# Block transposes of a cross-attention batch moved from steps 8 and 12 to steps 13 and 21

## The reference

```
x = layernorm(x + self_attention(x))            # 4 heads of 64
x = layernorm(x + cross_attention(x, ctx))      # 16 query heads of 128, 8 key heads, 1500 keys of width 128
x = layernorm(x + mixture_of_experts(x))        # 8 experts, 2 chosen, and a shared one
```

```
scores[h, q, s] = q[h, q, :] . k[h, s, :] / sqrt(128), masked      # 16 heads x 56 queries = 896 rows, 1500 keys
out             = softmax(scores) @ v, then a projection with Wo
```

## Time and profile before

| | |
|---|---|
| runs shown | 1952.05 and 1953.82 us, median 1952.93 |
| profiled execution | 1952.05 us, span 1950.2 us |
| mean granted TensorE clock | 0.93 |
| busy, share of the span | PE 85%, DVE 61%, ACT 53%, POOL 49% |
| DMA | 291.22 MB, 149 GB/s on average; queue of SP 53.3% of 16 engines |

### The profile page before, as it was taken

The page is one execution under the profiler, slowest core; times in us unless marked ns, Lnnn a source line. Parts: engine busy times, 40 slices in busy tenths (PEclk is TensorE's granted clock), DMA queues, the critical chain, the costliest instruction groups (busy, mean ns, idle before and its releaser), DMA issues.

```text
span 1950.2 us, 26771 instructions
## 1 busy us (share of the span) xinstructions
PE 1661.2 (85%) x8882; PEld 1431.6 (73%) x8882; DVE 1199.1 (61%) x3102; ACT 1033.4 (53%) x1780; POOL 946.3 (49%) x790
## 2 busy tenths in 40 slices
PE   8999788787979797878797878797988897869896
PEld 7988677676767676767676767676767676758896
DVE  5556665666666666666666666566666666547447
ACT  5443465655555555555555556555555555434452
POOL 1210354555555555555555555555555555344635
PEclk9999899999989898989898989898999898989999
DMA  4335866666666666666666666666676665533333
GB/s 174 114 129 181 197 162 154 162 154 160 157 158 157 160 158 158 156 162 158 159 152 157 155 153 157 152 157 152 157 153 157 152 158 124 135 127 105 102 97 101
DMA packets 171973, 291.22 MB, mean 149 GB/s; under 512 B 44702, under 2 KB 138560, under 8 KB 171712
## 3 DMA queue, kind: packets, MB, share of 16 engines
q1 hardware_dynamic: 129904, 266.49, 53.3%
q10 hardware_dynamic: 38912, 14.80, 3.2%
q0 software_dynamic: 3024, 8.26, 1.6%
HBM read 189.11 MB, written 100.38 MB: 148 GB/s over the span
## 4 chain that ended last, share of the span: by engine, by line
DMA 28%; PE 19%; POOL 14%; DVE 11%; issue 7%; ACT 6%; SPq 4%; ACTq 0%; DVEq 0%; POOLq 0%
DMA p_store<-b_by_block 26%; POOL b_keyed_over L1247 9%; POOL b_c_raw_over L1235 4%; DVE b_by_block L1093 3%; SPq L796 3%; DVE b_pT_lo L1098 2%; ACT b_p L975 2%; DVE b_p L1072 2%; PE b_turn L882 2%; PE b_score L868 2%; PE b_score L870 2%; PE b_score L869 2%; PE b_out L916 2%; PE c_gate L1647 2%; ACT b_pT_hi L961 2%
## 5 line engine op out<-in xcount | busy, mean ns | idle before, releaser
L1072 DVE CUSTOM_DVE_ANT_0 b_p<-b_score,b_mask_add 128x500 f32<-128x500 f32 x672 | 450.5, 671 | 358.4 <-PE b_score L870 237.3
L1247 POOL TENSOR_TENSOR b_keyed_over<-b_keyed,b_pT_hi 125x384 fp32r<-125x384 f32 x372 | 367.8, 1010 | 481.4 <-ACT b_pT_hi L968 480.9
L961 ACT CAST b_pT_hi<-b_turn 125x512 fp32r<-125x512 f32 x384 | 224.1, 585 | 366.4 <-PE b_turn L882 346.7
L900 PE MATMUL b_out<-b_pT_hi,b_c_hi 125*128 125x512 f32 x384 | 193.5, 504 | 208.8 <-DVE b_pT_lo L1098 208.7
L975 ACT ACTIVATE b_p<-b_p,b_shift 128x1500 f32<-128x1500 f32 x224 | 347.2, 1550 | 24.6 <-DVE b_top_min L1081 24.6
L968 ACT CAST b_pT_hi<-b_keyed 125x384 fp32r<-125x384 f32 x384 | 187.4, 507 | 234.3 <-PE b_out L902 121.8
L1098 DVE TENSOR_TENSOR b_pT_lo<-b_turn,b_pT_hi 125x512 fp32r<-125x512 f32 x384 | 264.0, 688 | 61.5 <-ACT b_pT_hi L961 61.0
L868 PE MATMUL b_score<-b_cT_hi,b_q_hi 128*128 128x500 f32 x672 | 275.3, 410 | 9.3 <-issue 7.5
L869 PE MATMUL b_score<-b_cT_lo,b_q_hi 128*128 128x500 f32 x672 | 272.1, 405 | 0.0
L870 PE MATMUL b_score<-b_cT_hi,b_q_lo 128*128 128x500 f32 x672 | 270.7, 403 | 0.0
L1093 DVE STREAM_TRANSPOSE b_by_block<-b_p 128x1536 f32<-128x1536 f32 x96 | 170.1, 1771 | 132.4 <-DMA p_store<-b_by_block 132.4
(11 more groups left out here) (261 smaller groups left out, 3242.0 us busy)
## 6 DMA issues: line engine op xcount, KB each, us to landing
p_store<-b_by_block SPq DMA_DIRECT2D x384, 192.0 KB, 8.8
b_keyed<-p_store SPq DMA_DIRECT2D x96, 768.0 KB, 14.5
cT_in<-in_ctxT SPq DMA_DIRECT2D x32, 750.0 KB, 7.0
b_c_raw<-in_ctx SPq DMA_DIRECT2D x32, 750.0 KB
q_store<-a_fold_in_or_q_stage SPq DMA_DIRECT2D x16, 896.0 KB, 4.2
q_in<-q_store SPq DMA_DIRECT2D x32, 448.0 KB, 17.9
b_rden_all<-rden_store ACTq DMA_DIRECT2D x32, 256.0 KB, 8.7
b_rden_all<-rden_store ACTq DMA_DIRECT2D x32, 192.0 KB, 6.5
```

The source lines that it names most:

```text
L900: pe.matmul(out, hi, pT_hi[:, c % 3, 0:w], start=(c == 0), stop=False)
L961: act.copy(pT_hi[:, c % 3, 0:w], turn_bank[c % 3][0:CK, 0:w]).then_inc(hi_done, 1)
L1072: dve.tensor_tensor_reduce(out=row(m, u)[:, keys], in0=score_bank[j][:, 0:FW], in1=mask_add[:, b, keys], scale=1.0, scalar=-3.0e38, op0=AL ...
L1247: pool.tensor_tensor(keyed_chunk(keyed_lo, c), keyed_chunk(keyed, c), by_blocks(pT_hi[:, c % 3, 0:128 * EVEN]).bitcast(F32), ALU.subtract) ...
```

## The change

The second and third transposes of a batch stand at steps 13 and 21 of VectorE's stream, where they stood at 8 and 12. The first stays at step 5. On SP the store of the third unit, `store_p(m, 2)`, stands behind the loads of the context and mask two batches ahead, and behind the store of a finished pair and the load of the residual, where it stood in front of all of these. No instruction is added or removed, and all shapes stay.

```diff
@@ phase_b
-        BLOCKS_AT = (5, 8, 12)
+        BLOCKS_AT = (5, 13, 21)
@@ sync(sp), in the loop over m
                 if m:
                     store_p(m, 1)
-                store_p(m, 2)
                 if m + 2 < B:
                     load_cT(m + 2)
                     load_mask(m + 2)
                 if m % 2 and m >= 3:
                     store((m - 3) // 2)
                     residual((m - 1) // 2)
+                store_p(m, 2)
```

## The result

The changed kernel takes **1839.19 us** (median of two runs, 1832.9 to 1845.48) against 1952.93: a ratio of 0.9418 with the 95% interval 0.9278 to 0.9557. The forecast was 1841. On another chip the pair gave 0.9394 [0.9368, 0.9421]. The kernel before differs by up to 2.4% between them, and another kernel need not differ by the same share, so ratios from different chips are not compared more finely than that.

What follows compares the result with a forecast made beforehand. The bound was taken as a cycle of waits, chiefly unit 2's transpose at step 12 on unit 0's late store. Plain batches 92 plus projecting 45 minus transposes 26 gave 111 us off 1952.05: 1841 us, range 1785 to 1905.

Steps and rivals of the forecast that it cites:

- The wait at step 12: VectorE's transpose of unit 2 waiting for unit 0's store to free its buffer; 132.4 us over all transposes, taken to zero.
- Plain batches: Even m: period from 47.6 to 41.5 us, 6.1 us in each of 15, 92 us gained before the transposes' cost.
- Projecting batches: Odd m, 48 more matmuls in steps 9 to 12: period 47.6 to 44.4 us, 45 us in 14 batches.
- rival A: `cT` lands late in projecting batches and takes their gain; 1886 us, or 1918 with transposes more exposed; 17%.
- t: Time in us since SP issues a batch's three `keyed` loads; one such issue to the next is one batch.
- What decides in plain batches: ScalarE's rounding of `c_raw` (L1007, step 15), waiting for its DMA: after t = 22.7, `c_raw` coming 0.9 us earlier.
- Unit 2's store: On SP before the third `keyed` load: lands in 3.2 us, about 2 us before that load wants it.
- Rival B: Unit 2's store lands late (17.6 us), delaying the third `keyed` load; decides from t = 6.1; period 54.0, 2138 us; 7%.
- The moved transposes: 64 transposes at steps 13 and 21 cost 0.9 us a batch (bounds nothing to 3.5), 26 us in 29 batches.
- L900's wait: TensorE standing for a late last `pT_lo`, 208.7 us before; to fall under a quarter, with one at L916 instead.
- Rival C: The wait moves with the transpose, or another fixed stretch keeps the period; 1945 us; 5%.
- rival D: All waits close and TensorE alone bounds: 40.2 us a period, 1737 us; 5%.

Runs made afterwards that it cites:

- the second profile: The changed kernel run once more, unaltered, on another chip: 1797.46 us, ratio 0.9394 to the kernel before.
- `cT` early: Against the changed kernel, the loads of `cT` and the mask also moved ahead of unit 1's stores: 1834.78 us, ratio 0.9611 to the kernel before.

## Why the prediction was right, and where it was not

**The wait at step 12 goes: right.** 132.4 us became 0.3, and moving the third transpose is enough for it. The order alone leaves 101.9 us of it (on another chip).

**Plain batches: right in size.** With the share of the transposes the working put them at 42.4 us; they took 41.7, and 39.7 in the second profile. From the first, 15 x 5.94 = 89 us of the gain.

**Projecting batches: too hopeful by a third.** Put at 45.3 with the transposes, they took 46.0, a gain of 14 x 1.6 = 22 us and not 32 (45.2 in the second profile). Here rival A's mechanism is at work: in the batch shown `cT` is issued at t = 32.4 (the working had about 31), lands 11.8 us later, and ScalarE waits. The working knew both landings, 6.6 and 12.3, said that the cover was thin, and left the wait out of the sum. A's price, though, was 45 us; with the wait taken away (`cT` early) they take 44.9, so as an estimate across chips it costs 1.1 x 14 = 15 us in the first profile and 0.3 x 14 = 4 in the second. The two kinds' errors, 89 us against 15 x 5.2 = 78 and 22 against 32, cancel in the periods, which is luck and no merit of the working. Outside them the first issue came 5.4 us later than before, and the profiled executions differ by 1952.05 - 1845.48 = 106.6.

**What decides in plain batches: right number, wrong route.** The rounding of `c_raw` was to start at t = 22.7; in the batch shown it starts 22.6 us after the first `keyed` issue. But not because `c_raw` has more room: SP issues it at t = 7.9 and no longer at 1.4. The announced sign failed: L1007's wait for `c_raw` was to grow over 50.8 us, and it fell to 12.7 us in 11 waits. In the batch shown `c_raw` is taken 1.0 us earlier in its period than in the earlier trace rows (t = 22.6 for 23.6), and ScalarE is ready for it 1.7 us later (t = 22.0 for 20.3); what keeps ScalarE back was not singled out.

**Unit 2's store: the step that failed.** The working had it land 3.2 us after its last issue and 2 us before SP wants it. In the batch shown it lands after 11.0, and the third `keyed` load is 7.0 us behind the first on average (1.4 before). The rule named in "DMA: Bandwidth & Descriptors" of the Trainium skill, section Specifications, on transfers under 512 B, pointed to this, and the trace agrees as to the place. As the explanation the rule does not do: runs of 12, 16 and 128 bytes are under 512 B too, and with them the late landings are gone. Rival B's price did not follow, though its point was passed: the third load at t = 7.0 is past t = 6.1, and B's sum, 7.0 + 41.5, would make a period of 48.5 us; it is 43.8. B shifted everything behind the load by its full lateness. But `c_raw`, issued 6.5 us later than before, lands in 14.7 us, and took some 22 before (issued 1.3 us behind 1033.92, taken at 1057.48), so that nothing of the lateness is left at its rounding. With the 4-byte pieces gone (runs of 12 and 16 bytes) the third load is 1.1 us behind the first, and the kernel takes 1758.35 us where the change took 1797.46 on the same chip: these stores cost it 2.2% there.

**The moved transposes: within the bounds.** 0.9 us a batch was taken. The nearest measure is the pair with short landings: with the store in 128-byte runs the change takes 38.5 and 45.3 us, the old steps 40.1 and 45.3. Moved transposes cost the projecting batches nothing that shows there; the plain ones gain 1.6 us there even so, and no run isolates what they pay.

**L900's wait** was to fall under a quarter of 208.7, 52; it fell to 62.3 in the first profile, which misses the sign, and to 31.8 in the second. The one at L916 took its place as said.

**Rival C** (the period stays) and **rival D** (TensorE alone bounds) are out. D's 40.2 us a period is reached as a mean of neither profile of the change (43.8 and 42.4); even with all DMA waits gone it is 41.4.

## What to carry to other kernels

When a store lands late, ask what else is in the DMA engines before rearranging who waits for it: here the change worked around a landing of 17.6 us for 6%, and removing its cause, 4-byte pieces of another store, gives 8% without moving a step. Moving an instruction and moving the queue entries that feed from it are one edit: each half alone was level or slower. With that cause gone the rearranging still brings 1.4%. And after any shift of VectorE against GpSimd, compare the durations of untouched instructions, because an engine kept out looks busy.

## What the runs showed of the hardware

**Stores in 4-byte pieces hold up the large transfers behind them.** The two stores of a batch carry 384 and 512 values. In the kernel before the `keyed` loads land after 14.5 us (median), with the same values in 128-byte runs after 5.9; in the changed kernel after 11.8 (second profile), and in runs of 12 and 16 bytes after 6.0. The first ten microseconds of a batch move 30 GB/s and 319. Not every transfer suffers: `cT`, which is issued late in the batch, lands after 7.0 us (median) in the kernel before and 6.9 with the 128-byte runs. The page's DMA part, the queue of these stores (packets, MB, share of the 16 engines; it also carries their loads), in the kernel before and then with the 128-byte runs:

```profile
q10 hardware_dynamic: 38912, 14.80, 3.2%
```

```profile
q10 hardware_dynamic: 17664, 15.73, 4.1%
```

By its share of the engines the queue did not look guilty: 3.2%, and 4.1% when the trouble was gone. The time stands in the records of others. Three stretches: the 4-byte pieces at 1032 to 1034 us of the kernel before, the queue of the `keyed` loads in the ten microseconds from 1034 on, and the same queue at 905.1 to 915.1 us with the 128-byte runs:

```profile
q10 hardware_dynamic: 528, 0.00, 12.6%
...
q1 hardware_dynamic: 46, 0.28, 78.9%
...
q1 hardware_dynamic: 784, 3.11, 85.9%
```

The pieces' own records are over before the first `keyed` packet starts, and they hold the 16 engines for 12.6% of 2 us. Then 46 packets hold them for 78.9% of 10 us, some 2.7 us a packet, where 784 packets with 128-byte runs take under 0.2 us each. How the pieces slow the packets behind them, the trace does not show. In both cures the number of pieces fell too, from 384 and 512 to 128 a store, so whether their size or their number does it is open.

**GpSimd can keep VectorE out through many instructions.** `norm_out`, 0.41 us by itself, took 8.2 us in 15 of 16 instances, through the ends of eight gapless GpSimd operations, all inside one record. Elsewhere it got in sooner: after 1.16 us with `norm_out` two steps later, after 0.41 to 1.52 us in the kernel before, while GpSimd's train ran on for some 4 to 9 us more. Wherever it took 0.5 us or longer, in these three kernels, it ended 0.15 us behind the end of a GpSimd operation. "SBUF — State Buffer" of the Trainium skill, section "Who interferes with whom", says that the two engines share a pair of ports under an exclusive lock. The trace agrees with an exclusion that ends with a GpSimd operation; which end lets VectorE in, the next one or that of the whole train, no run here singles out.
